# Two hardware loops over the sequences, on every engine, written out as straight programs

## The reference, cut to what matters

```
x = x + 0.5 * ffn(layernorm(x))        # stack 0: two layers
x = x + attention(layernorm(x))        # one head, all 1024 keys
x = x + 0.5 * ffn(layernorm(x))        # stack 1: the same two layers again

ffn, for each of 2 layers:
    h = shift_token(x)                              # half of the channels come from the token before
    q, k, v = split(h @ wqkv)                       # 8 heads of 64
    q, k = rotary(l2norm(q) * qs), rotary(l2norm(k) * ks)
    x = x + local_attention(q, k, v) @ wo           # windows of 64: a query sees its own and the one before
    h = layernorm(shift_token(x)) * g + b
    a, g = split(h @ w1 + b1)
    x = x + (a * gelu(g)) @ w2 + b2
```

## Time and profile before

| what | value |
|---|---|
| median of 3 runs | 1983.12 us (1982.61 to 1985.06) |
| the profiled execution's own time | 1988.07 us |
| its span, first to last instruction | 1986.3 us |
| mean granted TensorE clock | 0.932 of full speed |
| busy share: TensorE matmul, VectorE, ScalarE, GpSimd | 80%, 73%, 58%, 55% |

### The profile page before, as it was taken

One profiled execution on the slowest core, in us unless ns is written; L12 is line 12 of the kernel. 1 busy time (PEld: TensorE's weight loads), 2 busy tenths in 40 slices (PEclk: granted clock), 3 DMA queues, 4 the chain that ended last, 5 costly groups with the idle time before them and its releaser, 6 DMA issues.

```text
span 1986.3 us, 48409 instructions
## 1 busy us (share of the span) xinstructions
PE 1595.8 (80%) x15864; PEld 1273.2 (64%) x15864; DVE 1448.2 (73%) x3769; ACT 1151.8 (58%) x3315; POOL 1091.6 (55%) x1090
## 2 busy tenths in 40 slices
PE   1788989888989899746746858989897889898984
PEld 1576777766777777525535546777776777777763
DVE  6787869676869697455665648969686869787873
ACT  1576767565767686412213217868575668676771
POOL 2775748474858585321231236848475648576660
PEclk9899999999999999978978869999999999999997
DMA  7231212132212121041010022212123222112113
GB/s 259 49 113 45 47 41 56 48 83 65 47 42 48 40 54 38 13 131 43 0 42 21 0 77 47 53 42 47 43 56 85 50 62 47 44 45 50 38 38 109
DMA packets 183671, 112.13 MB, mean 56 GB/s; under 512 B 86720, under 2 KB 164128, under 8 KB 182944
## 3 DMA queue, kind: packets, MB, share of 16 engines
q1 hardware_dynamic: 183456, 109.12, 20.9%
HBM read 43.41 MB, written 23.42 MB: 34 GB/s over the span
## 4 chain that ended last, share of the span: by engine, by line
PE 53%; DVE 13%; ACT 13%; issue 9%; SPq 4%; POOL 4%; DMA 3%; DVEq 0%; ACTq 0%; POOLq 0%
PE QK L345 11%; PE OB L645 7%; ACT probs L1098 7%; PE TT L578 5%; PE SC L619 5%; PE VB L345 4%; DVE top L888 3%; PE QK L578 3%; PE TT L345 3%; PE OB L745 2%; PE VB L745 2%; PE SC L601 2%; ACT oT L1092 2%; PE SC L782 2%; PE VB L803 1%
## 5 line engine op out<-in xcount | busy, mean ns | idle before, releaser
L1098 ACT ACTIVATE probs<-SC,shift,qgain 128x128 f32<-128x128 f32 x1024 | 460.6, 480 | 102.1 <-DVE shift L896 101.9
L1222 POOL TENSOR_TENSOR ve<-mv,epsilon 128x1 f32<-128x1 f32 x128 | 24.5, 191 | 492.1 <-DVE mv L940 492.1
L345 PE MATMUL QK<-w_qkv,hT 128*128 128x512 f32 x768 | 228.3, 436 | 19.2 <-DMA w_qkv<-qkv_d 10.8
L1098 ACT ACTIVATION_READ_ACCUMULATOR probs<-SC,shift,qgain 128x1 f32 x1024 | 230.6, 225 | 0.0
L1235 POOL TENSOR_TENSOR rnorm<-clip,mhalf 128x8 f32<-128x8 f32 x128 | 211.4, 1652 | 12.1 <-DVE clip L905 11.9
L578 PE MATMUL TT<-ident,probs 128*128 128x128 f32 x1280 | 194.7, 280 | 27.4 <-ACT probs L1098 20.4
L888 DVE TENSOR_REDUCE top<-SC 128x4 f32<-128x512 f32 x256 | 174.9, 683 | 54.8 <-PE SC L619 54.7
L1244 POOL TENSOR_TENSOR qgain<-clip,mhalf 128x8 f32<-128x8 f32 x128 | 209.5, 1637 | 0.0
L949 DVE TENSOR_TENSOR rope_c<-QK,rope 128x512 f32<-128x512 f32 x256 | 172.3, 673 | 41.8 <-PE QK L345 41.3
L578 PEld LDWEIGHTS TT<-ident,probs 128*128 128x128 f32 x1280 | 154.7, 144 | 68.7 <-issue 21.6
L1249 POOL TENSOR_TENSOR q_r<-rope_c,rope_s 128x512 f32<-128x512 f32 x128 | 163.6, 1278 | 48.4 <-DVE rope_s L954 48.1
(11 more groups left out here) (136 smaller groups left out, 3858.8 us busy)
## 6 DMA issues: line engine op xcount, KB each, us to landing
v_prev<-v_own SPq DMA_DIRECT2D x256, 128.0 KB, 2.3
x_att<-stream SPq DMA_DIRECT2D x128, 64.0 KB, 2.1
h<-stream SPq DMA_DIRECT2D x256, 32.0 KB, 1.9
stream<-x_new SPq DMA_DIRECT2D x32, 256.0 KB
w_qkv<-qkv_d SPq DMA_DIRECT2D x3, 1536.0 KB, 6.5
h<-x_mid SPq DMA_DIRECT2D x128, 32.0 KB
h<-x_mid SPq DMA_DIRECT2D x128, 31.8 KB
rope<-rope_d SPq DMA_DIRECT2D x24, 128.0 KB, 2.7
```

Of the source, the lines that this page charges most:

```text
L345: last = mm(dst, fr(left(a)), fr(right(b)), start=(k == 0), stop=(k == 2))
L1098: last = nc.scalar.activation(probs[:, b, hd, :], SC[:, hd * P:hd * P + P], ACT.Exp, bias=shift[:, b, hd:hd + 1], scale=qgain[:, b, hd % 4 ...
```

## The change

The hardware loops over a stack's passes are gone on all engines. `pipeline` calls `step` for every step from 0 to the last with plain numbers, and `Tile.count` gives a constant in every case, so that each wait of the stacks is on a constant. SyncE's passes are written out as well, its addresses in memory being constants. The order of work on each engine, the buffers, the waits themselves and the transfers stay what they were. The attention's loop between the stacks stays as well.

```diff
 class Tile:
-    def __init__(self, it, c, stack):
-        self.it, self.c = it, c
+    def __init__(self, c, stack):
+        self.c = c
         self.i = c % TILES
         self.first = stack * NT
     def count(self, back=0, every=1, unit=1):
-        c = self.c - back + self.first
-        k = (c // every + 1) * unit
-        return k if self.it is None else self.it * (TILES // every * unit) + k
+        return ((self.c - back + self.first) // every + 1) * unit
...
-def pipeline(eng, step, stack):
+def pipeline(step, stack):
...
-    for g in range(TILES):
-        step(tile_of(None, g), burst_of(None, g), None)
-    with eng.Fori(1, ITERS) as it:
-        for j in range(TILES):
-            step(tile_of(it, j), burst_of(it, j), burst_of(it, j - 1))
-    for g in range(NT, LAST + 2):
-        step(tile_of(None, g), burst_of(None, g), burst_of(None, g - 1))
+    for g in range(LAST + 2):
+        step(tile_of(g), burst_of(g), burst_of(g - 1))
...
@@ SyncE
-                iteration(None, 0, 0, 0, None, None)
+                iteration(0)
...
-                with sp.Fori(1, SEQS - 1) as it:
-                    iteration(it, 0, 0, it, 0, it - 1)
+                for n in range(1, SEQS - 1):
+                    iteration(n)
...
-                with sp.Fori(SEQS + 1, ITERS) as it:
-                    iteration(it, 0, 1, it - SEQS, 1, it - SEQS - 1)
+                for n in range(SEQS + 1, ITERS):
+                    iteration(n)
```

More of the change, by code:

```diff
@@ L61, in count, with tile_of, burst_of @@
     def count(self, back=0, every=1, unit=1):
-        c = self.c - back + self.first
-        k = (c // every + 1) * unit
-        return k if self.it is None else self.it * (TILES // every * unit) + k
+        return ((self.c - back + self.first) // every + 1) * unit
     def loads(self):
-        k = self.c // TILES
-        layer = (k if self.it is None else self.it + k) // SEQS
-        return layer + (self.first // NT * DEPTH + 1)
+        return self.c // TILES // SEQS + (self.first // NT * DEPTH + 1)
 def need(eng, sem, count):
-    if not isinstance(count, int) or count > 0:
+    if count > 0:
         eng.wait_ge(sem, count)
-def pipeline(eng, step, stack):
-    def tile_of(it, g):
+def pipeline(step, stack):
+    def tile_of(g):
         def f(skew):
             c = g - skew
-            if it is None and not 0 <= c < NT:
-                return None
-            return Tile(it, c, stack)
-        return f
-    def burst_of(it, g):
-        if (g - BURST) % TILES or (it is None and g < BURST):
-            return None
-        n = (g - BURST) // TILES + stack * ITERS
-        return n if it is None else it + n
-    for g in range(TILES):
-        step(tile_of(None, g), burst_of(None, g), None)
-    with eng.Fori(1, ITERS) as it:
-        for j in range(TILES):
-            step(tile_of(it, j), burst_of(it, j), burst_of(it, j - 1))
-    for g in range(NT, LAST + 2):
-        step(tile_of(None, g), burst_of(None, g), burst_of(None, g - 1))
+            return Tile(c, stack) if 0 <= c < NT else None
+        return f
+    def burst_of(g):
+        if (g - BURST) % TILES or g < BURST:
+            return None
+        return (g - BURST) // TILES + stack * ITERS
+    for g in range(LAST + 2):
+        step(tile_of(g), burst_of(g), burst_of(g - 1))
 def build(nc, x_in, w_attn, b_attn, kq_gain, v_gain, wqkv, qk_gain, wo_in, ln_gb, w1_in, b1_in, w2_in,
@@ L452, in stack, with iteration @@
                 first = k * ITERS
-                def iteration(it, c, l, s, lb, sb_, at=(), after_burst=None):
+                def iteration(n, at=(), after_burst=None):
+                    l, s = divmod(n, SEQS)
                     for j in range(TILES):
                         def tile(skew):
[L458 to L465, removed]
+                            c = n * TILES + j - skew
+                            return Tile(c, k) if 0 <= c < NT else None
+                        if j == 0 and l > 0:
+                            need(sp, s_st, (first - 1 + n) * 32 + 16)
+                        loads(tile(0), l, s)
                         for when, do in at:
@@ L469, in iteration @@
                         moves(tile)
-                        if j == BURST - TILES and lb is not None:
-                            store(lb, sb_, (c // TILES if it is None else it) - 1 + first)
+                        if j == BURST - TILES and n:
+                            lb, sb_ = divmod(n - 1, SEQS)
+                            store(lb, sb_, n - 1 + first)
                             if after_burst:
@@ L509, in rope_after @@
                     return do
-                iteration(None, m, 0, SEQS - 1, 0, SEQS - 2,
-                          [(i + 3, rope_after(i)) for i in range(TILES - 3)])
+                iteration(SEQS - 1, [(i + 3, rope_after(i)) for i in range(TILES - 3)])
                 def after_qkv():
@@ L520, in after_wo @@
                     load_wo(1)
-                iteration(None, m + TILES, 1, 0, 0, SEQS - 1,
-                          [(0, rope_after(5)), (1, rope_after(6)), (2, after_qkv), (2, rope_after(7)), (6, after_wo)],
+                iteration(SEQS, [(0, rope_after(5)), (1, rope_after(6)), (2, after_qkv), (2, rope_after(7)), (6, after_wo)],
                           lambda: load_ffn(1))
-                with sp.Fori(SEQS + 1, ITERS) as it:
-                    iteration(it, 0, 1, it - SEQS, 1, it - SEQS - 1)
+                for n in range(SEQS + 1, ITERS):
+                    iteration(n)
                 for g in range(NT, LAST + 1):
-                    moves(lambda skew: Tile(None, g - skew, k) if 0 <= g - skew < NT else None)
+                    moves(lambda skew: Tile(g - skew, k) if 0 <= g - skew < NT else None)
                 store(1, SEQS - 1, first + ITERS - 1)
@@ L672, in f @@
                         pe.wait_ge(s_vlo[b], t.count(every=2, unit=16))
-                        if t.it is not None or t.c > 0:
+                        if t.c > 0:
                             pe.wait_ge(s_vup[1 - b], t.count(back=1, every=2, unit=16))
@@ L752, in ffn @@
                 w2_half(1)
-            pipeline(pe, step(0), 0)
+            pipeline(step(0), 0)
             stack_done(pe, 0)
@@ L805, in _ @@
                 pe.wait_ge(g_x2, s * TILES + TILES)
-            pipeline(pe, step(1), 1)
+            pipeline(step(1), 1)
         @block.vector
@@ L1009, in step @@
                                                in1=gelu[0:m, k % 2, :], op0=ALU.add, op1=ALU.mult).then_inc(s_act2, 1)
-            pipeline(dve, step, 0)
+            pipeline(step, 0)
             stack_done(dve, 0)
@@ L1080, in _ @@
                 normalise(x_new, x_2, LN_OUT).then_inc(g_y, 1)
-            pipeline(dve, step, 1)
+            pipeline(step, 1)
             for s in range(SEQS):
@@ L1117, in step @@
                     need(act, s_o, t.count(back=TILES - 1))
-                    if t.it is not None or t.c >= 2:
+                    if t.c >= 2:
                         act.wait_ge(s_vlo[b], t.count(back=2, every=2, unit=16))
@@ L1165, in _ @@
             act.wait_ge(s_zero, ZEROED)
-            pipeline(act, step, 0)
+            pipeline(step, 0)
             stack_done(act, 0)
@@ L1192, in _ @@
                              TT[:, 512:1024].rearrange("k (h q) -> k h q", h=4)).then_inc(g_pTa, 1)
-            pipeline(act, step, 1)
+            pipeline(step, 1)
         @block.gpsimd
@@ L1251, in step @@
                     g.tensor_tensor(k_a[:], rope_c[:, 512:1024], rope_s[:, 512:1024], ALU.add).then_inc(s_ka, 1)
-            pipeline(pool, step, 0)
+            pipeline(step, 0)
             stack_done(pool, 0)
@@ L1270, in _ @@
                 rstd(LN_OUT, s * 5 + (SEQS + 5))
-            pipeline(pool, step, 1)
+            pipeline(step, 1)
 ZEROED = 5
```

## The result

The changed kernel takes 1925.5 us (median of 4 runs, 1924.96 to 1927.37), the kernel before 1982.9 us in the runs beside them: a ratio of 0.9713, with a 95% interval of 0.9696 to 0.973. Later, in five rounds together, it was 0.9708 (0.9695 to 0.9721). The gain is 57 to 58 us; 65.5 us were forecast, and the stated range of 1902 to 1934 us holds the time.

A forecast was written before the change was run, and what follows sets the result against it. TensorE and VectorE take turns without slack, with TensorE stalling at twelve jumps back. Twelve pairs, 290.63 - 12 x 18.76 = 65.5 us gained, other terms nothing: 1983.1 - 65.5 = 1917.6 us, range 1902 to 1934 us.

The forecast's parts named there:

- the twelve idle times: TensorE's "issue" time before the k_r transposes, 42.0 us in 12 pieces, laid to the stacks' twelve jumps back.
- the low clock behind the stall: After each jump TensorE's slow clock and disturbed order cost 2.0 us a pair, 23.5 us in all.
- The split of 42.0 and 23.5 us: The 65.5 us gain at the passages: 42.0 us stall itself, 23.5 us low clock and disturbed order afterwards.
- The written-out passage as a control: Passage from step 63 to 64, without a jump, takes 18.76 us a pair; the twelve with jumps should match it.
- VectorE's refetch is the next limit: VectorE idles 13.3 us after its branch in stack 1; adds nothing here, but limits if only TensorE's jump went.
- Registers at the waits at nothing: Removing register arithmetic at TensorE's and VectorE's waits counted as no gain; 22 us if all were exposed.
- Streaming at nothing: Fetching the longer straight code from memory counted as no cost; 100 us lost at the far end.
- the dry stream: Rival: TensorE's straight code is fetched late, 0.9 us per packet, 100 us lost, 2018 us; chance of slower 0.05.
- the sum's last step, the subtraction from the median: The 65.5 us read in the profiled execution (1988.07 us) taken off the runs' median, 1983.1 us, giving 1917.6 us.

The follow-up runs named there:

- one-pass loops: Kernel before, with the seven-pass loop on TensorE, VectorE, ScalarE and GpSimd replaced by seven loops of one pass each; 1928.8 us, ratio 0.9709.
- two-pass body: Kernel before, with each loop body holding two passes on all engines, so TensorE jumps back 4 times in place of 12; 1944.6 us, ratio 0.9791.
- the hint: Kernel with everything but TensorE written out, plus a hint naming the branch's target in each pass of TensorE's loop; twelve pairs 244.2 us, from 289.0.
- the two kernels with idle time only: Changed kernel with one added TensorE wait before the k_r transposes at twelve passages, long in one, short in the other; 1972.3 and 1955.8 us.
- the short kernel: Changed kernel with an added TensorE wait for GpSimd's k_a before the k_r transposes at twelve passages; 1955.8 us, ratio 0.9839.
- the kernel with only TensorE's loop: Changed kernel with TensorE given its loop back, all other engines and SyncE written out; 1989.7 us, ratio 1.0021 against the kernel before.
- the attention's edit: Changed kernel with the attention's loop over the four sequences written out too, on all engines; 1926.7 us, ratio 0.9706 against the kernel before.

## Why the prediction was right, and where it was short

**What bounds the kernel, and the reading of the twelve idle times:** right. The count of twelve, the branch's duration and the idle time belong together, and the experiments show that the cause is the fetch of the target: no jump, no cost (one-pass loops); a third of the jumps, 28% of the cost over the twelve pairs (two-pass body); the same jumps with their target announced, also 28% (the hint).

**The second part of the price, the low clock behind the stall:** right, and it is shown apart from the jump by the two kernels with idle time only. The split of 42.0 and 23.5 us was about right: TensorE's idle time before `k_r` is gone but for 0.9 us, and its busy time in the pairs fell from 229.96 to 205.93 us, by 24.0. In the short kernel it is 1.0 us for an idle time of 1.4, and 1.7 us for the low clock in six of ten cases. That the clock falls at every passage, as it did in the trace of before, is not a rule: the two kernels show passages with 1.4 to 2.3 us of idle time where it stayed.

**The written-out passage as a control:** right to 1%. I took 18.76 us a pair; the twelve take 18.92 us on average. The two pairs at the change of layer, which had no control of their own, take 19.34 and 19.23 us. This makes 63.6 us in place of 65.5. The control pairs themselves took 19.2 and 18.9 us in the changed kernel, 18.83 and 18.69 before, so agreement to 1% is as good as they repeat.

**VectorE's refetch is the next limit:** right. TensorE alone written out gives the kernel 1938 us, and the loss against 1926 us lies in stack 1.

**Registers at the waits at nothing:** right. All three tests (the other engines' with TensorE alone written out, TensorE's with the hint, the attention's) show no gain from constants, within some 4 us where 22 us were the far end. **Streaming at nothing:** right. The trace after has no idle time of the kind behind the dry stream in the stacks, and fewer packets on TensorE's queue.

**The term that was mis-sized** is the sum's last step, the subtraction from the median: 65.5 us forecast, 57.3 measured. In the two profiled executions the spans differ by 63.1 us, 2.4 us short of the sum. Of the terms outside the pairs the largest is the burst step at stack 1's change of layer, 29.94 us after and 26.97 us before:

```profile
1576.76:1603.73 26.97, 22.54 (x191) 18.59 (x190) 16.79 (x34) 14.35 (x38) 10.67 (x11) 1.00 0.14 37
```

TensorE waited for `w_o` in both (2.5 and 2.9 us), but before, the clock stayed at 1.00 that time. The five-step stretches before the burst steps are 0.1 to 0.2 us longer after than before, over twelve of them some 2 us. These losses are largely made up elsewhere: the eight steps from the first transposes of `k_r` on took 4.1 us less, both stacks together. The remaining 5 to 6 us are in the reference. The profiled execution of before, in which the pairs were read, took 1988.07 us, that of after 1925.34 us, which is its median. I had taken the 4.95 us between profile and median for an offset that both kernels have; the kernel after has none. The four runs of the kernel before beside the result took 1980.3 to 1985.1 us and the nine of the repeated comparison 1980.3 to 1987.4 us, so the profiled one was longer than all of these. Among the 21 runs beside the other experiments, which took 1980.7 to 1990.7 us, five are as long. So the forecast took a gain that it had read in a long execution off the median of shorter ones. Where in it the 5 us lie can't be said from one trace: the twelve pairs of the kernel with only TensorE's loop, 289.0 us, were hardly shorter.

**What is left open:** why executions of the same kernel spread over 7 us, and why its median moved from 1982.9 to 1987.0 us between rounds. The experiments ran on three different chips (medians of the kernel before 1986.2, 1987.0 and 1983.9 us), so times of different experiments are compared by their ratios. The stretch from stack 0's last `k_r` to stack 1's first, which only the attention's edit touches, is 377.4 to 383.3 us long in the profiles of this study, and its time at low clock 137 to 160 us; what decides it wasn't tested. Nor is it known why the five-step stretches take about 46.3 us at some places and 46.7 us at others; both occur within one kernel, behind passages with a pause and without.

## What to carry to other kernels

Look for idle times of "issue" whose count is that of a loop's jumps, and read the branch's own duration on each engine: a body that the engine has to fetch anew costs microseconds for each jump, one that stays on it some tenths. Where part of the program is already written out, the same passage there is the control, and here it gave the time of a passage to 1% and the gain at the passages to 3%. Price an idle time on TensorE with the slow clock that can follow it, and read a forecast's sum against several executions: the distance of one profile from the median may be chance.

## What the runs showed of the hardware

TensorE's comparing branch took 3.3 to 3.9 us where it jumped to code that had to be fetched, 208 to 239 ns in the attention's short loop, and 67 to 88 ns where it fell through. VectorE, ScalarE and GpSimd showed 34 to 67 ns in each case, yet VectorE stood idle for 2.0 to 2.6 us behind six of its twelve jumps; a branch's own duration doesn't tell all. With a hint at the head of the body TensorE's took 1.07 to 1.38 us in one stack and 0.45 to 0.48 us in the other.

The Trainium skill, Runtime: NRT & Kernel Launch, section on instruction fetch mechanics, says that a taken branch out of the fetched window waits for its target's page, and that straight code is fetched ahead; the runs agree, with 3.4 us for the former and no visible cost for the latter.

That TensorE's clock was at half speed after the stalls was known from the trace of before. That it falls after an idle time of 1.4 us too, in six of ten equal cases (0.92 against 1.00 over the pair), and not in one of 2.5 us at a change of layer, nor in two of 2.1 and 2.3 us at passages, I had not expected.
